# Attention and feed-forward on one core: TensorE's step regrouped into two long fp32r runs, with all queues and the drain reordered

## The chip, the cores and the metric

One core of one Trainium2 chip runs the whole program. The metric is the device time of one execution in microseconds, as the median of several runs. The change touches no arithmetic: the same products are formed in another order.

## What is computed

Input `x` is 128 batches of 32 tokens with 512 features, 4096 tokens in all. Cut to what matters:

```python
# style: one 32x32 matrix per batch, picked by a style number
h = einsum('bct,bcd->bdt', x, weights[style])
q, k, v = split(clip(h @ w_qkv.T, -8, 8))        # 32 heads of 16
q, k = layer_norm(q), layer_norm(k)
p = softmax(where(causal, q @ k.T / 4 + alibi, -inf))
x = x + (p @ v) @ w_out.T
# adapter: one 512x512 matrix per batch, picked by an adapter number
y = einsum('bsi,boi->bso', x, weight[adapter])
shared = relu(y @ up) ** 2 @ down
routed = (y @ fc1 @ expert) * sum(top2(y @ gate)) @ fc2
x = x + layer_norm(shared + routed)
```

## The kernel before

Engines: TensorE (PE) multiplies, VectorE (DVE) and ScalarE (ACT) read PSUM and round, GpSimd (POOL) works in SBUF only and issues the gathers and scatters, SyncE (SP) issues the other transfers. Each engine's queue is written out by hand; between them stand semaphores, and `upto(e, name, t)` makes engine `e` wait until event `name` has happened for tile `t`.

The tokens are sorted by style into 32 tiles of 128 (`T = 32`), and by adapter into 38 slots of 128. An fp32 product is made of three fp32r products (high with high, high with low, low with high), each 128x128 by 128x512. In the program's words ACT makes the high part (`high_...`), DVE or POOL the low part (`low_...`).

**The attention stage** is a software pipeline over `i`. In step `i` TensorE forms, for several tiles at once: `style(i+1)`; the three projections `project(i, ...)` (Q, K and V, 12 fp32r matmuls each, L586); `values(i-4)` (L604, 96 small bf16 matmuls); `turn_slot` (transposes of gathered rows, L663) and `adapt_slot(i-6)` (12 fp32r matmuls, L677); `turn_values(i-4)` (L616), `turn_qk(i-1)` twice (L636); `scores(i-2)` (L651, 96 small bf16 matmuls); `out_project(i-4)` (12 fp32r matmuls, L628). Values and scores are each issued as two halves of 48 matmuls, put between fp32r groups. The PSUM banks are `B2` (Q, adapter), `B3` (K, Q turned), `B4` (values turned), `B5` (V, K turned), `B6` (output projection), `B7` (style, slot turned) and `pair` (scores, values).

The chain of one tile behind TensorE: scores, `bias_max` (DVE L1215, L1219), `subtract_max` (POOL L1559), `soft_exp` (ACT L963), `turn_probs` (DVE L1287), `high_probs` (ACT L968) and `low_probs` (POOL L1571), values, `divide` (DVE L1236, L1240), `turn_values`, `high_o` and `low_o`, output projection, `add_x` (x1). The heads' K and V are spread into block form by SP (`spread_k` to `kx`, `spread_v` to `vx`). In the background 20 chunks of feed-forward weights are split into high and low parts and kept in memory (`load_chunk`, `high_chunk`, `low_chunk`, `keep_chunk`), and the adapted rows are scattered to `y_rows`.

**The drain** is what follows step 31: the last tiles' scores, values and output projections, with the first five `up` groups of the feed-forward stage between them. **The feed-forward stage** runs over 8 groups of 512 tokens: 8 times `up` (L741), `gate_products` of the next group (L710), 4 times `down` (L758, L765), and two adapter slots per group. The rows of a group come transposed in halves of 16 bits (`load_y`), are joined to words (`join_y`), and are split (`high_y` on ACT, `low_y` on DVE) before `up` and `gate_products` of that group can run. In group 0 the splits of group 1 are spread over `up` 5, 6 and 7:

```python
        return {5: (0,), 6: (1,), 7: (2, 3)}[f]
```

## Time and profile before

| | us |
|---|---|
| median of 3 runs | 1157.25 (1157.22 to 1161.35) |
| profiled execution | 1158.09 |
| its span, first to last instruction | 1156.3 |
| TensorE busy in the span | 1113.8 (96%) |
| GpSimd, VectorE, ScalarE busy | 709.5, 679.8, 604.2 |
| mean granted TensorE clock | 0.989 |

The profiled execution took 1158.09 us, 1.8 us more than its span; it is 0.84 us above the median of the runs. Matmuls overlap, so a busy TensorE is not one at its peak: the distances between starts tell what a matmul costs in a row of them. The attention stage with its start fills the first 604 us, the drain lies between 604 and 650 us, and from there the feed-forward groups follow.

### The profile page before, as it was taken

How to read it: one execution, taken by the hardware profiler on the slowest of the kernel's cores; microseconds unless marked ns; L12 is line 12 of the kernel's file. 1: busy time of each engine (PE TensorE's matmuls, PEld its weight loads, DVE VectorE, ACT ScalarE, POOL GpSimd, SP SyncE). 2: the span in 40 equal slices, each digit the busy share in tenths (PEclk: the TensorE clock that was granted, in tenths of full speed). 3: DMA queues.
4: the chain of work that ended last, by engine and by line, in shares of the span. 5: the costliest groups of instructions: out<-in, count | busy, mean ns of one | idle time of the engine just before them, and what ended most of it. 6: DMA issues, size and time to landing. Idle time of an engine off the chain costs nothing.

```text
span 1156.3 us, 27340 instructions
## 1 busy us (share of the span) xinstructions
PE 1113.8 (96%) x10996; PEld 885.7 (77%) x10996; DVE 679.8 (59%) x1050; ACT 604.2 (52%) x1009; POOL 709.5 (61%) x610
## 2 busy tenths in 40 slices
PE   6999999999999999999998889999999999999994
PEld 4777777777777777777776668787888878787883
DVE  5767565756575657565667336655656556554532
ACT  4466767676767676757575532516162534424120
POOL 3466787878787878787764445645545454533332
PEclk9999999999999999999998989999999999999998
DMA  6135545454545454436468923241513313130101
GB/s 260 39 95 177 203 158 195 161 201 157 200 158 199 160 197 149 156 125 166 122 189 196 325 90 92 79 140 55 140 65 99 89 67 104 40 83 28 46 28 36
DMA packets 90796, 152.38 MB, mean 132 GB/s; under 512 B 46000, under 2 KB 46768, under 8 KB 85296
## 3 DMA queue, kind: packets, MB, share of 16 engines
q1 hardware_dynamic: 73024, 105.84, 28.8%
q0 software_dynamic: 12224, 34.10, 9.1%
q10 hardware_dynamic: 5424, 10.71, 2.7%
q8 instruction: 88, 1.44, 0.5%
q14 instruction: 36, 0.29, 0.1%
HBM read 89.78 MB, written 38.27 MB: 111 GB/s over the span
## 4 chain that ended last, share of the span: by engine, by line
PE 92%; DVE 3%; DMA 2%; ACT 1%; issue 1%; POOL 1%; SPq 0%; DVEq 0%; ACTq 0%; POOLq 0%
PE bank L586 22%; PE pair L765 15%; PE bank L741 14%; PE bank L677 9%; PE bank L628 8%; PE bank L758 8%; PE bank L576 3%; PE pair L651 3%; PE pair L604 3%; PE bank L636 2%; PE bank L663 2%; PE bank L710 1%; PE bank L616 1%; DMA x_rows<-x1t 1%; DMA stage<-in_wqkv 0%
## 5 line engine op out<-in xcount | busy, mean ns | idle before, releaser
L1565 POOL TENSOR_TENSOR w_lo<-w2t,w_hi 128x2048 fp32r<-128x2048 f32 x38 | 175.5, 4619 | 8.1 <-ACT w_hi L910 7.9
L586 PE MATMUL bank<-wqkv_hi,h_hi 128*128 128x512 f32 x384 | 158.8, 414 | 0.5 <-issue 0.4
L1619 POOL TENSOR_TENSOR u_lo<-act,u_hi 128x512 fp32r<-128x512 f32 x64 | 82.8, 1294 | 112.1 <-ACT u_hi L1097 112.0
L586 PE MATMUL bank<-wqkv_hi,h_lo 128*128 128x512 f32 x384 | 150.6, 392 | 0.0
L586 PE MATMUL bank<-wqkv_lo,h_hi 128*128 128x512 f32 x384 | 149.6, 390 | 0.0
L741 PE MATMUL bank<-yT_hi,up_hi 128*128 128x512 f32 x256 | 101.1, 395 | 0.3 <-DVE yT_lo L1259 0.3
L765 PE MATMUL pair<-down_hi,u_hi 128*128 128x512 f32 x256 | 100.9, 394 | 0.0
L765 PE MATMUL pair<-down_hi,u_lo 128*128 128x512 f32 x256 | 100.8, 394 | 0.0
L765 PE MATMUL pair<-down_lo,u_hi 128*128 128x512 f32 x256 | 100.3, 392 | 0.0
L741 PE MATMUL bank<-yT_lo,up_hi 128*128 128x512 f32 x256 | 99.8, 390 | 0.0
L741 PE MATMUL bank<-yT_hi,up_lo 128*128 128x512 f32 x256 | 99.7, 390 | 0.0
L1422 DVE TENSOR_TENSOR act<-act 128x512 f32<-128x512 f32 x59 | 67.5, 1143 | 50.2 <-ACT act L1093 50.2
L1657 POOL TENSOR_SCALAR fve<-fmv 128x1 f32<-128x1 f32 x32 | 22.8, 712 | 115.6 <-DVE fmv L1477 115.5
L1187 ACT ACTIVATE total<-bank,weight 128x512 f32<-128x512 f32 x32 | 21.9, 684 | 126.6 <-PE bank L758 126.6
L1559 POOL TENSOR_TENSOR probs<-probs,row_max 128x1024 f32<-128x1024 f32 x32 | 61.2, 1911 | 40.4 <-DVE row_max L1219 40.3
L586 PEld LDWEIGHTS bank<-wqkv_hi,h_lo 128*128 128x128 f32 x384 | 72.0, 188 | 16.5
L586 PEld LDWEIGHTS bank<-wqkv_hi,h_hi 128*128 128x128 f32 x384 | 72.2, 188 | 16.0 <-issue 1.7
L586 PEld LDWEIGHTS bank<-wqkv_lo,h_hi 128*128 128x128 f32 x384 | 72.4, 189 | 13.0 <-issue 0.2
L910 ACT ACTIVATE w_hi<-w2t 128x2048 fp32r<-128x2048 f32 x38 | 73.3, 1930 | 13.4 <-DMA w2t<-in_w 13.3
L1571 POOL TENSOR_TENSOR p_lo<-probsT,p_hi 128x1024 bf16<-128x1024 f32 x32 | 68.8, 2150 | 15.3 <-ACT p_hi L968 14.6
L1093 ACT ACTIVATE act<-bank 128x512 f32<-128x512 f32 x64 | 37.8, 591 | 71.0 <-PE bank L741 70.8
L1472 DVE TENSOR_TENSOR total<-total,pair 128x512 f32<-128x512 f32 x32 | 21.9, 684 | 89.4 <-PE pair L765 89.4
(179 smaller groups left out, 2965.8 us busy)
## 6 DMA issues: line engine op xcount, KB each, us to landing
w2t<-in_w SPq DMA_DIRECT2D x38, 1024.0 KB, 4.8
vx<-v_hl SPq DMA_DIRECT2D x128, 68.0 KB
x_rows<-x1t SPq DMA_DIRECT2D x32, 256.0 KB, 3.0
x1g<-x_rows SPq DMA_DIRECT2D x32, 256.0 KB, 3.1
kx<-k_hl SPq DMA_DIRECT2D x124, 64.0 KB
ffn_high<-w_high SPq DMA_DIRECT2D x20, 256.0 KB, 3.1
ffn_low<-w_low SPq DMA_DIRECT2D x20, 256.0 KB, 3.0
stage<-in_wqkv SPq DMA_DIRECT2D x3, 1024.0 KB, 7.9
```

The lines of the kernel that those rows point to most:

```text
L586: m = e.matmul(into, a[:, c, :], b[:, n, c, :], start=(c == 0 and k == 0), stop=(c == KC - 1 and k == 2))
L628: m = e.matmul(B6, a[:, j, :], b[:, j, :], start=(j == 0 and k == 0), stop=(j == BPT - 1 and k == 2))
L677: m = e.matmul(into, a[:, P * c:P * c + P], b[:, c, :], start=(c == 0 and k == 0), stop=(c == KC - 1 and k == 2))
L741: i = e.matmul((B2, B3)[n % 2], a[:, w, cols], b[m % 2][:, c, :], start=(c == 0 and k == 0), stop=(c == KC - 1 and k == 2))
L758: i = e.matmul((B6, B7)[n % 2], a[m % 2][:, c, toks], b[:, c, :], start=(c == 0 and k == 0), stop=(c == KC - 1 and k == 2))
L765: i = e.matmul(pair[:, n % 2, :], a[f][:, toks], b[:, f, :], start=(f == 0 and k == 0), stop=(f == FC - 1 and k == 2))
L910: e.activation(w2_hi[:, :, :], w2t[:, :, :], ACT.Copy).then_inc(d_whi, 1)
L1422: e.tensor_tensor(act[n % 2][:, :], act[n % 2][:, :], act[n % 2][:, :], ALU.mult) \
L1559: e.tensor_tensor(probs[:, :, :], probs[:, :, :], row_max[:, :].rearrange("p (h o) -> p h o", o=1) .broadcast_to([P, HEADS, SEQ]), ALU.sub ...
L1565: e.tensor_tensor(w2_lo[:, :, :], w2t[:, :, :], w2_hi[:, :, :].bitcast(F32), ALU.subtract).then_inc(d_wlo, 1)
L1571: e.tensor_tensor(p_lo[:, :], probsT[:, :], p_hi[:, :], ALU.subtract).then_inc(A["plo"], 1)
L1619: e.tensor_tensor(u_lo[n % FC][:, :], act[n % 2][:, :], u_hi[n % FC][:, :].bitcast(F32), ALU.subtract) \
```

## The change

TensorE's step `i` now reads: Q, K, V projections of tile `i` in a row (36 fp32r matmuls); `turn_slot(i-6)`, `turn_values(i-4)`, `turn_q(i-1)`, `turn_k(i-1)`; `style(i+1)`; the whole of `scores(i-2)`; `adapt_slot(i-6)` and `out_project(i-4)` in a row (24 fp32r matmuls); the whole of `values(i-3)`, which was `values(i-4)` in the middle of the step. Style moves from bank `B7` to `B6`. The loop has one step fewer, step 31 being written into the drain. The core of the diff, TensorE first:

```diff
-            def values(t, half):
+            def values(t):
-            def scores(t, half):
+            def scores(t):
...
+            for i in range(T - 1):
+                project_q(i)
+                if i < SHORT:
                     style(i + 1)
...
+                project_k(i)
+                project_v(i)
+                if i >= LAG:
                     turn_slot(i - LAG, B7)
+                if i >= 4:
                     turn_values(i - 4)
+                if i >= 1:
+                    turn_q(i - 1)
+                    turn_k(i - 1)
+                if i >= SHORT:
+                    style(i + 1)
+                if i >= 2:
+                    scores(i - 2)
+                if i >= LAG:
                     adapt_slot(i - LAG, B2)
+                if i >= 4:
                     out_project(i - 4)
+                if i >= 3:
+                    values(i - 3)
```

The drain on TensorE after the change:

```python
project_q(T - 1); project_k(T - 1); project_v(T - 1)
turn_slot(LAST, B7); turn_values(T - 5); turn_k(T - 2); turn_q(T - 2)
scores(T - 3); adapt_slot(LAST, B2)
turn_qk(T - 1, q ...); turn_qk(T - 1, k ...)
values(T - 4); out_project(T - 5); turn_values(T - 4); scores(T - 2)
out_project(T - 4); values(T - 3); up(0, 0); turn_values(T - 3)
scores(T - 1); up(0, 1); values(T - 2); out_project(T - 3)
turn_values(T - 2); up(0, 2); out_project(T - 2); values(T - 1)
up(0, 3); turn_values(T - 1); up(0, 4); out_project(T - 1)
gate_products(0)
```

The other queues follow. POOL's step:

```diff
             for i in range(T):
+                upto(e, "o", i - 4)
+                if i > LAG:
+                    scatter_slot(i - LAG - 1)
...
+                if i + 3 < T:
+                    gather_x(i + 3)
+                    gather_style(i + 3)
+                if i >= LAG:
+                    low_w2(i - LAG)
+                reciprocals(i)
+                if i >= 3:
+                    low_probs(i - 3)
+                if i >= LAG - 1:
+                    upto(e, "s", i - 2)
+                    gather_slot(i - LAG + 1)
+                if i >= 2:
+                    subtract_max(i - 2)
+                low_v(i)
+                if i + 2 < T:
+                    style(i + 2)
```

VectorE's step becomes: `turn_probs(i-3)`, `divide(i-4)`, clip and statistics of Q, `low_chunk(i-5)`, clip and statistics of K, aggregate, clip of V, `low_slot`, `low_o(i-4)`, `low_h(i+1)`, `bias_max(i-2)`, `low_q` and `low_k(i-1)`, `add_x(i-4)`. ScalarE's: `high_probs(i-3)`, `high_w2`, `high_chunk(i-5)`, `normalize(i-1)`, `slot_in`, `high_o(i-4)`, `high_v(i)`, `high_h(i+1)`, scaling and high parts of Q and K of tile `i-1`, `slot_out`, `soft_exp(i-2)`. SP's: `spread_v(i-3)`, `store_x1(i-5)`, `keep_chunk(i-5)`, `load_chunk(i-4)`, `load_w2(i-5)`, `spread_k(i-1)`.

For group 1 the words are joined by VectorE in the drain, into a region of their own (`words_second`, laid over `yt`), and all four splits follow `up` 5 of group 0:

```diff
-        return {5: (0,), 6: (1,), 7: (2, 3)}[f]
+        return range(KC) if f == EARLY else ()
...
+            for c in range(KC):
+                join_y(1, c)
+            add_x(T - 2)
             divide(T - 1)
```

What that moves, in the queues as they are built. TensorE before, from the V projection of a middle step to the next step's first projection (L586 projection, L616 values turned, L636 Q or K turned, L677 adapter, L651 scores, L628 output projection, L576 style, L604 values):

```order
L663 MATMUL bank<-cst,xg 128x128 x4
...
L616 MATMUL bank<-cst,on 128x128 x4
L636 MATMUL bank<-cst,qn 128x128 x4
L677 MATMUL bank<-w_hi,xgT_hi 128x512
...
L636 MATMUL bank<-cst,kn 128x128 x4
L651 MATMUL pair<-kx,q_hi 32x128 x8
...
L628 MATMUL bank<-wo_hi,o_hi 128x512
...
L576 MATMUL bank<-style_bd,xt 128x128 x4
```

TensorE after the change, the same place (L592 projection, L667 slot turned, L620 values turned, L640 Q and K turned, L582 style, L654 scores, L681 adapter):

```order
L592 MATMUL bank<-wqkv_hi,h_lo 128x512
L667 MATMUL bank<-cst,xg 128x128 x4
L620 MATMUL bank<-cst,on 128x128 x4
L640 MATMUL bank<-cst,qn 128x128 x4
L640 MATMUL bank<-cst,kn 128x128 x4
L582 MATMUL bank<-style_bd,xt 128x128 x4
L654 MATMUL pair<-kx,q_hi 32x128 x8
...
L681 MATMUL bank<-w_hi,xgT_hi 128x512
```

All turns, style and the scores now stand in one stretch between the two fp32r runs; the adapter moved behind the scores.

ScalarE before, in group 0 from the copy of the gates on (L1093 relu, L948 words joined, L953 high part of the words, L1097 high part of u, L906 slot in):

```order
L959 ACTIVATE gates<-bank 16x512
L1093 ACTIVATE act<-bank 128x512
L948 ACTIVATE y_words<-yt_first 128x512 x2
L953 ACTIVATE yT_hi<-y_words 128x512
L1097 ACTIVATE u_hi<-act 128x512
L906 ACTIVATE xgT_hi<-bank 128x512
```

ScalarE after the change, the same place (L1103 relu, L969 high part of the words, L1107 high part of u, L920 slot in, L975 gates):

```order
L975 ACTIVATE gates<-bank 16x512
L1103 ACTIVATE act<-bank 128x512
L969 ACTIVATE yT_hi<-words_second 128x512 x4
L1107 ACTIVATE u_hi<-act 128x512
L920 ACTIVATE xgT_hi<-bank 128x512
```

The joining has left ScalarE here, and all four high parts of group 1 stand behind the first relu.

## Rows read from the trace of the kernel before

**Rows 1.** The page's chain that ended last: shares of the span by engine

```profile
PE 92%; DVE 3%; DMA 2%; ACT 1%; issue 1%; POOL 1%; SPq 0%; DVEq 0%; ACTq 0%; POOLq 0%
```

**Rows 2.** Windows: length, busy time of PE, PEld, DVE, ACT, POOL; granted clock, DMA

```profile
120.00:604.00 484.00, 483.74 (x6945) 384.71 (x6943) 311.09 (x526) 326.89 (x562) 386.56 (x318) 1.00 0.52 171
```

**Rows 3.** TensorE's waits: us in total, times, longest

```profile
PE bank L710 <- DVE yT_lo L1259: 5.3, 1, 5.3
PE pair L651 <- DVE on L1240: 3.9, 1, 3.9
PE pair L604 <- DVE probs L1215: 2.3, 1, 2.3
...
PE bank L677 <- DVE xgT_lo L1208: 1.5, 1, 1.5
PE pair L604 <- POOL p_lo L1571: 1.0, 1, 1.0
```

**Rows 4.** Timeline of TensorE, a middle step: start, length, instruction, count

```profile
412.50 0.47 PE L586 MATMUL bank<-wqkv_hi,h_hi 128*128 128x512 f32 x1
...
415.44 0.22 PE L604 MATMUL pair<-vx,p_hi 128*32 128x68 bf16 x4
...
416.00 0.47 PE L586 MATMUL bank<-wqkv_hi,h_hi 128*128 128x512 f32 x1
...
418.93 0.22 PE L604 MATMUL pair<-vx,p_hi 128*32 128x68 bf16 x4
...
419.44 0.66 PE L663 MATMUL bank<-cst,xg 128*128 128x128 f32 x4
...
426.33 0.60 PE L636 MATMUL bank<-cst,kn 128*128 128x128 f32 x4
426.86 0.25 PE L651 MATMUL pair<-kx,q_hi 64*32 64x128 bf16 x8
...
427.39 0.50 PE L628 MATMUL bank<-wo_hi,o_hi 128*128 128x512 f32 x1
...
430.38 0.25 PE L651 MATMUL pair<-kx,q_hi 64*32 64x128 bf16 x8
...
430.95 1.13 PE L576 MATMUL bank<-style_bd,xt 128*128 128x128 f32 x8
431.84 0.48 PE L586 MATMUL bank<-wqkv_hi,h_hi 128*128 128x512 f32 x1
```

**Rows 5.** Timeline of TensorE: whole bursts, scores at the start, values in the drain

```profile
53.65 0.25 PE L651 MATMUL pair<-kx,q_hi 64*32 64x128 bf16 x8
...
54.58 1.16 PE L576 MATMUL bank<-style_bd,xt 128*128 128x128 f32 x8
...
632.32 0.39 PE L628 MATMUL bank<-wo_hi,o_lo 128*128 128x512 f32 x1
632.64 0.22 PE L604 MATMUL pair<-vx,p_hi 128*32 128x68 bf16 x4
...
633.54 0.50 PE L741 MATMUL bank<-yT_hi,up_hi 128*128 128x512 f32 x1
```

**Rows 6.** Timeline of TensorE: step 31 begins, gate products end, first down begins

```profile
585.63 0.47 PE L586 MATMUL bank<-wqkv_hi,h_hi 128*128 128x512 f32 x1
...
649.43 0.40 PE L710 MATMUL bank<-yT_lo,gate_hl 128*16 128x512 f32 x1
...
672.81 0.78 PE L758 MATMUL bank<-route_hi,yT_hi 128*128 128x512 f32 x1
```

**Rows 7.** Windows as rows 2: a stretch without fp32r at the start, two after waits

```profile
52.60:55.50 2.90, 2.90 (x115) 2.59 (x112) 2.41 (x7) 1.90 (x5) 0.88 (x3) 1.00 0.03 6
...
612.20:615.20 3.00, 2.61 (x101) 2.04 (x101) 2.86 (x4) 1.14 (x4) 0.00 (x0) 0.50 0.90 77
...
668.70:673.80 5.10, 5.09 (x14) 2.73 (x15) 0.00 (x0) 1.46 (x2) 3.15 (x3) 0.50 0.33 102
```

**Rows 8.** Timeline of ScalarE in the drain: four high parts of words

```profile
607.14 2.18 ACT L953 ACTIVATE yT_hi<-words_first 128x512 fp32r<-128x512 f32 x4
```

More of the change, by code:

```diff
@@ L377, in words @@
     def words(m, c):
-        return y_words[m % 2][:, c, :] if m else words_first[:, UP_CHUNKS // KC * c + 1, :]
+        if m == 0:
+            return words_first[:, UP_CHUNKS // KC * c + 1, :]
+        return words_second[:, c, :] if m == 1 else y_words[m % 2][:, c, :]
     def halves(word, n):
@@ L403, in route_bank @@
     def route_bank(c):
-        return pair[:, 0, :] if c == 0 else B6
+        return pair[:, 0, :] if c == 0 else B7
     def last_slot(m):
@@ L783, in _, with project_q @@
                          start=True, stop=True)
-            e.matmul(B6[0:1, 0:SLOTS], idc[:, :], onehot[:, 0::BPT], start=True, stop=True) \
+            e.matmul(B7[0:1, 0:SLOTS], idc[:, :], onehot[:, 0::BPT], start=True, stop=True) \
                 .then_inc(s_tp, 1)
             make_route(0)
-            for i in range(T):
-                live = lambda t: 0 <= t < T
-                slot = i >= LAG
-                if 0 < i < T - 1:
-                    style(i + 1)
-                if live(i):
-                    upto(e, "cq", i - 1)
-                    if i > LAG:
-                        e.wait_ge(d_mc, i - LAG)
-                    project(i, 0, B2, "pq")
-                if i == 0:
-                    style(1)
+            def project_q(i):
+                upto(e, "cq", i - 1)
+                if i > LAG:
+                    e.wait_ge(d_mc, i - LAG)
+                project(i, 0, B2, "pq")
@@ L845, in _ @@
+            turn_q(T - 2)
+            scores(T - 3)
+            adapt_slot(LAST, B2)
+            e.wait_ge(d_tl, LAST + 1)
+            turn_qk(T - 1, qn[(T - 1) % 2], "qn", B7, "tq")
+            upto(e, "khi", T - 2)
+            upto(e, "klo", T - 2)
+            turn_qk(T - 1, kn[(T - 1) % 2], "kn", B5, "tk")
+            values(T - 4)
+            out_project(T - 5)
             turn_values(T - 4)
+            scores(T - 2)
+            out_project(T - 4)
+            values(T - 3)
             up(0, 0)
-            out_project(T - 4)
@@ L848, in _ @@
-            values(T - 3, 0)
-            values(T - 3, 1)
+            turn_values(T - 3)
+            scores(T - 1)
             up(0, 1)
-            turn_values(T - 3)
-            scores(T - 1, 0)
-            scores(T - 1, 1)
+            values(T - 2)
+            out_project(T - 3)
+            turn_values(T - 2)
             up(0, 2)
-            out_project(T - 3)
-            values(T - 2, 0)
-            values(T - 2, 1)
+            out_project(T - 2)
+            values(T - 1)
             up(0, 3)
-            turn_values(T - 2)
@@ L860, in _ @@
-            values(T - 1, 0)
-            values(T - 1, 1)
-            out_project(T - 2)
             turn_values(T - 1)
@@ L1404, in _ @@
                 m.then_inc(A["aggr"], 1)
-                if 0 <= i - 4 < CHUNKS:
-                    low_chunk(i - 4)
-                if i == T - 1:
-                    e.wait_ge(f_y, 2 * KC * 16)
-                    for c in range(KC):
-                        join_y(c)
-                if live(i - 4):
+            for i in range(T - 1):
+                if i >= 3:
+                    turn_probs(i - 3)
+                if i >= 4:
+                    divide(i - 4)
+                take_q(i)
+                if i < SHORT:
+                    low_h(i + 1)
+                stats_of(i, 0, qn, "cq")
+                if i == 0:
+                    low_weights(3)
+                if 0 <= i - 5 < CHUNKS:
+                    low_chunk(i - 5)
+                take_k(i)
+                stats_of(i, 1, kn, "ck")
+                aggregate(i)
+                take_v(i)
+                if i >= LAG:
+                    low_slot(i - LAG, B7)
+                if i >= 4:
+                    low_o(i - 4)
+                if i >= SHORT:
+                    low_h(i + 1)
+                if i >= 2:
+                    bias_max(i - 2)
+                if i >= 1:
+                    low_q(i - 1, B3)
+                    low_k(i - 1, k_bank(i - 1), k_hl)
+                if i >= 4:
                     add_x(i - 4)
@@ L1607, in _, with low_v @@
                     .then_inc(A["shift"], 1)
+            def low_v(t):
                 upto(e, "vhi", t)
```

421 lines of the change are left out of this document (201 added, 220 removed).

## The prediction

> **What bounds the kernel now.** I read the chain of waits first: TensorE holds 92% of it, every other engine 3% or less [rows 1]. The windows say where: in the 484 us from 120 to 604 TensorE is busy for 483.74, GpSimd for 386.56, ScalarE for 326.89 and VectorE for 311.09 [rows 2]. So the attention stage has no wait to remove; there only what TensorE itself spends can change the time. The table of TensorE's waits then shows what is left outside that stage: 5.3, 3.9, 2.3, 1.5 and 1.0 us, each a single wait [rows 3]. By the timeline they lie between 604 and 669 us, in the drain and in group 0 of the feed-forward stage. Last, the timeline of one middle step: it lasts 431.84 - 412.50 = 19.34 us [rows 4]. The reader should see the distances between starts there. Twelve fp32r matmuls in a row stand about 0.23 us apart, but each passage to the small bf16 matmuls and back costs something over the matmuls themselves.
>
> **Part one, the regrouped step.** The count of matmuls stays the same, and so does the price of each. What goes is the halving of two bursts. Values: in the step the first half takes 416.00 - 415.44 = 0.56, the second 419.44 - 418.93 = 0.51 [rows 4]. A whole burst between two fp32r groups, in the drain, takes 633.54 - 632.64 = 0.90 [rows 5]. Going in costs 632.64 - 632.32 = 0.32 where the distance is otherwise 0.23, so 0.09 more, and the first fp32r matmul behind a burst has a distance about 0.1 longer. Two halves: 0.56 + 0.51 + 2 x 0.09 + about 0.1 = 1.35; one whole 0.90 + 0.09 + 0.1 = 1.09. That is 0.26 saved. Scores: the halves take 427.39 - 426.86 = 0.53 and 430.95 - 430.38 = 0.57 [rows 4], the whole 54.58 - 53.65 = 0.93 [rows 5]; with one entry (0.09) and one return (0.1) fewer, 0.17 + 0.19 = 0.36 is saved. The transposes cost the same 0.36 to 0.44 per group wherever they stand, beside fp32r or beside each other; so moving them is free. One passage is new, from style to bf16: the trace never has it. Its nearest row is the K transposes before scores, 426.86 - 426.33 = 0.53 [rows 4], about 0.1 above a group before other fp32 work; it may cost nothing, or 0.2. With 0.05 for it, I take 0.26 + 0.36 - 0.05 = 0.57 a step; the ends are 0.35 (my entry and return costs are seen only once each) and 0.70. Steps 4 to 30 have all of it: 27 x 0.57 = 15.4 us, from 9.5 to 19. The new step is 18.77 us. Values of tile 0 move from step 4 into step 3, and the last ones out of the drain; what one end gains the other pays.
>
> **Does anything else hold that step up?** I laid the queues out along one new step, 0 at its first Q matmul, with the durations of the trace: Q, K, V end at 8.4, the turns at 10.2, style at 11.2, scores at 12.1, adapter and output projection at 17.7, values at 18.7. VectorE: clip of V done at 9.2, and the K turn into the same bank starts at 9.7, a margin of 0.5 and the tightest of all. `bias_max` ends at 15.1. GpSimd starts at 0.2 (values of the step before), then scatter, two gathers, the adapter's low part (until 8.7), reciprocals, `low_probs` (12.4), one gather (13.7), then `subtract_max` from 15.1 to 17.1, `low_v` and style, end 18.7. It has 0.2 us to the next step, but 1.4 us of wait inside, so a late start is taken up. ScalarE ends with the exponential at 18.2. The exponential, the turn of the probabilities and both parts of them reach values with 5 us to spare. SP spreads K when its low part is there (16.7) and has until 12 of the next step. Each of these is hidden behind 18.77 us of TensorE; its cover is gone if the step falls below about 18.6. In front of the loop little changes; I put the start at zero, with 1 us either way.
>
> **Part two, the drain.** From step 31's first matmul to the end of the gate products of group 0 there are 649.66 - 585.63 = 64.0 us (the last gate matmul starts at 649.43 [rows 6]). Three waits, 3.9 + 2.3 + 1.0 = 7.2 us [rows 3], go in the new order, since more independent work stands before the last turns. With them goes the clock's fall: in 612.2 to 615.2, right behind the waits, the granted clock is 0.50, which is 1.2 GHz, against 1.00 (2.4 GHz) [rows 7]. Half of 3.0 us is 1.5. Step 31 also has its two halvings less, 0.6. Together 9.3. Laying the new queues out the same way gives new waits: `turn_values(28)` waits 0.35 for the quotient, which stands behind the word splits on VectorE; `out_project(28)` 1.0 for its low part, behind the exponential and the scaling of K on ScalarE; `scores(31)` waits for the spread K of the last tile, issued after its low part at 24.9 us from the start of step 31, over 2.5 us of issue and perhaps 2 of landing, 0.7 to 2, say 1. That is 2.3. Net 7.0 us; the ends are 1 (each new wait tripled) and 9.3.
>
> **Part three, group 0.** Before, `gate_products(1)` waited 5.3 us for the last low part of group 1's words [rows 3], because ScalarE joined and rounded them between the relus. The clock then stood at 0.50 for 5.1 us [rows 7], half of it lost: 2.5. Now VectorE joins them in the drain, and ScalarE's four high parts behind the first relu take 2.2 us [rows 8]. They are done some 6 us after the gate products of group 0, while TensorE comes to `gate_products(1)` only 13.6 us after them. So 5.3 + 2.5 = 7.8 goes. The 1.5 us for the adapter's low part [rows 3] stay: ahead of it ScalarE waits for the store of the last x1, and the four high parts fit in front of that store. What is late next is the weight transfer for `down`, or the low part of the adapter in `down` (about 1.4 us of margin after the transfer of its matrix); the first `down` starts today at 672.81 [rows 6]. So the ends are 4.5 and 7.8. From there to the end nothing changes but one store.
>
> **The sum.** 15.4 + 7.0 + 7.8 = 30.2 us. The profiled execution has 1158.09, which gives 1127.9; it stands 0.84 above the median, so on the scale of the runs 1157.25 - 30.2 = 1127.0. The parts' best ends, 19 + 9.3 + 7.8 = 36 and 1 for the start, give 1120; their worst, 9.5 + 1 + 4.5 = 15, give 1142.
>
> **The rivals.** *The drain keeps its waits in new places* (0.15). Against: the layout above. For: it is five hand-written queues, and one instruction late on any of them stops TensorE; a stop of a few us brings the clock's fall with it, as behind the waits of the old drain. Then part two is worth nothing or minus 3, and part three half: 1127 + 7 + 4 = 1138, 1134 to 1143.
>
> *Another engine sets the step* (0.12). GpSimd has 386.56 us of work in 484 [rows 2], 15.4 per 19.34 us step, plus its issue gaps; it now starts only when the previous values are done, and the softmax chain is tied to two waits inside the step. If the step stays at 19.34 us, the 15.4 us go: 1142. It takes 30.2 / 27 = 1.1 us of wait per step to lose everything. I put this between 1139 and 1155.
>
> *The clock falls in every step* (0.09), the way to slower. Before, no stretch without fp32r matmuls inside the steps is longer than scores and style, 431.84 - 430.38 = 1.46 us [rows 4], and the longest at the start, 2.9 us of turns, scores and style, ran at 1.00 [rows 7]. Now turns (4 x 0.44), style (1.0) and scores (0.9) stand together: 3.7 us in each step without one. Falls so far followed only idle time, and TensorE is not idle here; this speaks against it. If it fell, each would cost between the two losses seen, 1.5 and 2.5 us [rows 7]: 27 x 1.5 - 30 gives +10, 27 x 2.5 - 30 gives +38, so 1167 to 1195. It decides from 1.1 us per step on. The Trainium skill ("TensorE: Matmul & The Clock Gate", Part 4, PE-mode transpose) says that transposes don't count as TensorE activity the way matmuls do, so by that rule a stretch opened by four groups of transposes is where the clock would give way. By the rule the kernel would be slower than before, at about the 1167 to 1195 of this rival; the start's stretch at 1.00 is the only trace against it.
>
> **How the numbers follow.** The forecast, 1120 to 1134 about 1127, has 0.63; the drain 0.15, the engine-bound step 0.12, the clock 0.09, and 0.01 is left. The range leaves out the clock and the tail of the engine-bound step: 1118 to 1146. A measurement of this kernel tells about 0.5% from no change, 5.8 us. All of the forecast, the drain and most of the engine-bound step are faster by more: 0.87. Within 0.5%: 0.04. Slower: the clock, 0.09.
>
> **What would show it.** In the new profile: the middle step at 18.7 to 18.9 us between first Q matmuls, with the distance 0.23 unbroken over 36 matmuls; granted clock 1.00 from 120 to 585; no wait of TensorE in it for POOL or VectorE; step 31 to gate products in 56 to 58 us; no wait of `gate_products(1)` and no window at 0.50 behind it; the 1.5 us for the adapter still there. A step over 19.1 us, a clock under 0.95 in the attention stage, or drain waits over 6 us in sum would prove me wrong.

## The result and the profile after

| | before | after |
|---|---|---|
| median of 20 runs each, us | 1157.74 (1156.88 to 1161.35) | 1162.42 (1156.93 to 1171.22) |
| profiled execution, its span | 1158.09, 1156.3 | 1165.9, 1164.1 |
| mean granted clock | 0.989 | 0.986 |

The change makes the kernel slower, by a ratio of 1.0047 (95% interval 1.0029 to 1.0064), and its runs spread over 14 us, those of before over 4.5. The profiled execution of the change is one of the longer ones, 3.5 us above its median; the stretches below are of that one execution. Four marks in TensorE's timeline cut the two spans into five stretches: the first Q matmul of step 4, that of step 31, the last gate matmul of group 0 and the first routed product (the marks of the last three of before are in [rows 6]).

| stretch, us | before | after | difference | forecast |
|---|---|---|---|---|
| start, to step 4 | 68.33 | 80.45 | +12.12 | 0 |
| steps 4 to 30 | 517.30 | 513.12 | -4.18 | -15.4 |
| drain, to the last gate matmul | 63.80 | 68.97 | +5.17 | -7.0 |
| group 0, to its first routed product | 23.38 | 18.80 | -4.58 | -7.8 |
| the rest | 483.49 | 482.76 | -0.73 | 0 |

These add up to 7.8 us, the difference of the spans. The gains in the steps and in group 0 are there in part, and the start and the drain lost. First the chain that ended last in the changed kernel:

```profile
PE 84%; DMA 6%; issue 4%; DVE 4%; ACT 1%; SPq 1%; POOL 0%; DVEq 0%; POOLq 0%
```

TensorE had 92% of it [rows 1]; now transfers, issue and VectorE hold 14%, where they had 6. The windows (columns as in [rows 2]) show the attention stage and five short stretches behind waits:

```profile
120.00:590.00 470.00, 461.99 (x6771) 383.37 (x6771) 310.77 (x511) 325.24 (x560) 379.40 (x315) 1.00 0.54 170
607.00:612.00 5.00, 4.65 (x110) 3.96 (x111) 2.88 (x6) 4.16 (x10) 3.56 (x5) 0.66 0.62 161
634.00:638.00 4.00, 3.56 (x102) 2.98 (x103) 1.97 (x3) 0.00 (x0) 0.00 (x0) 0.57 1.09 337
672.00:677.00 5.00, 4.86 (x15) 3.94 (x16) 0.38 (x1) 1.03 (x2) 1.28 (x1) 0.68 0.00 0
36.00:41.00 5.00, 3.72 (x14) 3.40 (x15) 4.77 (x4) 1.64 (x3) 3.22 (x4) 0.66 0.21 59
65.00:72.00 7.00, 6.98 (x18) 4.62 (x19) 2.67 (x4) 3.14 (x5) 2.05 (x2) 0.57 0.49 142
```

In 470 us of attention TensorE was idle for 8, where it had been idle for 0.3 in 484 [rows 2]; the clock stayed at 1.00 there. Behind the long waits at the start, in the drain and in group 0 it fell; a value like 0.66 is the mean of a part at 0.50 (1.2 GHz) and a part at 1.00 (2.4 GHz). TensorE's table of waits over the whole span names what it waited for:

```profile
PE bank L582 <- issue: 8.4, 3, 4.3
PE bank L640 <- DVE vf L1222: 7.8, 7, 4.5
PE pair L654 <- DMA kx<-k_last: 4.3, 1, 4.3
PE bank L681 <- DVE xgT_lo L1233: 2.8, 1, 2.8
```

Compare [rows 3]: the waits of 5.3, 3.9 and 2.3 us are gone, three groups that were not there have come, and the adapter's 1.5 us have grown to 2.8. Each has its own cause.

**The start: GpSimd's style comes last in its step.** `issue` in the first row hides a wait for GpSimd. Timeline of GpSimd, then of TensorE, around the style product of tile 2:

```profile
34.19 0.23 POOL L1630 TENSOR_SCALAR var_eps<-mean_var 128x2 f32<-128x2 f32 x1 [7.07 <-DVE mean_var L1418]
...
35.65 1.12 POOL L1646 TENSOR_TENSOR v_hl<-vf,v_hl 128x512 bf16<-128x512 f32 x1
36.73 0.45 POOL L1552 TENSOR_TENSOR style_bd<-style_rows,cst 128x128 f32<-128x128 f32 x1
```

```profile
37.28 0.98 PE L582 MATMUL bank<-style_bd,xt 128*128 128x128 f32 x3 [4.28 <-issue]
```

The style operand needs nothing of the softmax chain, but it now stands in the queue behind the variance, for which GpSimd waited 7.07 us, and behind the low part of V. It ends at 37.18, and TensorE starts at 37.28 after 4.28 us idle. At tile 4 it happens again (3.2 us). The clock windows 36 to 41 at 0.66 and 65 to 72 at 0.57 are what follows.

**The steps: the w2 transfer shares its time with the spreads.** Undisturbed steps last 18.7 to 18.9 us, as forecast, but 10 of the 24 from step 7 on are over 19.0, up to 20.77. SP's timeline of one such step, then ScalarE's:

```profile
305.20 0.34 SPq L448 DMA_DIRECT2D w2t<-in_w  x1
305.72 3.52 SPq L501 DMA_DIRECT2D kx<-k_hl  x4
309.35 2.89 SPq L510 DMA_DIRECT2D vx<-v_hl  x4
```

```profile
313.62 1.92 ACT L924 ACTIVATE w_hi<-w2t 128x2048 fp32r<-128x2048 f32 x1 [3.40 <-DMA w2t<-in_w]
```

1 MB is issued at 305.20, the small pieces of both spreads right behind it, and ScalarE gets the matrix at 313.6, 8.4 us after its issue. Behind `w_hi` on ScalarE stand the feed-forward chunk and the scaling of Q and K; VectorE's `w_low` and V's clip come late in turn, and TensorE's K turn waits for that clip (seven waits in the second row above, six of them in the steps). From 120 to 590 us ScalarE waits 14 times for this matrix, 20.7 us in sum. In the trace of before it never does there: that order issues the w2 transfer by itself, behind the spreads.

**The drain: VectorE's joins meet GpSimd's long low part.** Timelines of VectorE and GpSimd:

```profile
597.91 5.85 DVE L1280 COPY words_first<-yt_first 128x512 uint16<-128x512 uint16 x4
603.66 0.67 DVE L1222 TENSOR_SCALAR kn<-bank 128x512 f32<-128x512 f32 x1
...
605.25 1.43 DVE L1280 COPY words_first<-yt_first 128x512 uint16<-128x512 uint16 x4
606.58 0.68 DVE L1222 TENSOR_SCALAR vf<-bank 128x512 f32<-128x512 f32 x1
```

```profile
598.62 4.82 POOL L1620 TENSOR_TENSOR w_lo<-w2t,w_hi 128x2048 fp32r<-128x2048 f32 x1 [3.13 <-ACT w_hi L924]
```

Four copies of halves to words take 1.43 us when GpSimd's long subtraction isn't running, 5.85 when its 4.82 us subtraction runs: the longest single one of the eight lasts 4.83 us, where their median is 0.45, and the four end 0.3 us after the subtraction ends (603.44). So one of them stood still for it. The Trainium skill ("SBUF — State Buffer", "SBUF: two separate sides") says that VectorE and GpSimd share one pair of ports to SBUF, and calls it "an exclusive lock, not a bandwidth split"; these rows agree. V's clip ends at 607.26 and TensorE's K turn starts at 607.31, after 4.45 us. Then the spread K of tile 31 (issued 624.70 to 627.91) meets the 2 MB of the odd half of the up weights, which ScalarE's queue issues at 626.62 and 627.02: 4.3 us.

One more stop of the drain isn't a wait for an operand. TensorE stops in the middle of a burst of values, whose operands it had waited for at the burst's start:

```profile
641.74 0.21 PE L609 MATMUL pair<-vx,p_lo 128*32 128x68 bf16 x2 [1.47 <-issue]
```

A like one, of 1.29 us, stands in the scores of step 6. A transfer of the DMA kind "instruction" stands in the DMA view of both places; the profile names no releaser, so the cause is not shown.

**Group 0.** The gate products of group 1 wait for nothing. But VectorE has all four low parts in a row now, and the adapter's stands behind them:

```profile
667.62 3.56 DVE L1287 TENSOR_TENSOR yT_lo<-words_second,yT_hi 128x512 fp32r<-128x512 f32 x4
671.10 0.68 DVE L1233 TENSOR_TENSOR xgT_lo<-bank,xgT_hi 128x512 fp32r<-128x512 f32 x1
```

so its wait grew from 1.5 [rows 3] to 2.8 us, with a window at 0.68 behind it. This fall of the clock isn't there in every execution: in the traces of two experiments below, e1 and e5, the same wait is followed by a clock of 1.00, and group 0 lasts 17.4 us in place of 18.8.

### The profile page after: what moved, and what is told of

Same layout as the page of the kernel before. It is cut to its first block, busy times and chain, and to the rows that moved or that the text cites. A ratio compares the mean times of both kernels' runs of the same rounds, so it can differ in the third digit from the quotient of the medians.

```text
span 1164.1 us, 27353 instructions
## 1 busy us (share of the span) xinstructions
PE 1103.2 (95%) x10996; PEld 895.4 (77%) x10996; DVE 696.3 (60%) x1058; ACT 602.2 (52%) x1001; POOL 711.1 (61%) x610
## 4 chain that ended last, share of the span: by engine, by line
PE 84%; DMA 6%; issue 4%; DVE 4%; ACT 1%; SPq 1%; POOL 0%; DVEq 0%; POOLq 0%
PE bank L592 18%; PE pair L768 15%; PE bank L744 15%; PE bank L681 9%; PE bank L761 8%; PE bank L632 6%; DMA w2t<-in_w 4%; PE bank L582 3%; PE pair L654 2%; PE bank L640 2%; PE pair L609 2%; PE bank L714 1%; PE bank L667 1%; PE bank L620 1%; DVE words_first L1280 1%
## 5 line engine op out<-in xcount | busy, mean ns | idle before, releaser
L592 PE MATMUL bank<-wqkv_hi,h_hi 128*128 128x512 f32 x384 | 154.8, 403 | 0.3
L592 PE MATMUL bank<-wqkv_lo,h_hi 128*128 128x512 f32 x384 | 150.0, 391 | 0.0
L592 PE MATMUL bank<-wqkv_hi,h_lo 128*128 128x512 f32 x384 | 149.9, 390 | 0.0
L592 PEld LDWEIGHTS bank<-wqkv_hi,h_hi 128*128 128x128 f32 x384 | 72.5, 189 | 17.6 <-issue 1.4
L592 PEld LDWEIGHTS bank<-wqkv_hi,h_lo 128*128 128x128 f32 x384 | 72.4, 188 | 15.4
L592 PEld LDWEIGHTS bank<-wqkv_lo,h_hi 128*128 128x128 f32 x384 | 72.5, 189 | 15.0 <-issue 1.2
L1103 ACT ACTIVATE act<-bank 128x512 f32<-128x512 f32 x64 | 37.8, 591 | 75.2 <-PE bank L744 75.1
```

The costliest lines, as they stand in the source:

```text
L592: m = e.matmul(into, a[:, c, :], b[:, n, c, :], start=(c == 0 and k == 0), stop=(c == KC - 1 and k == 2))
```

## The experiments

Medians stand with their ratio to the kernel before on the same chip. All but e4 and e8 mend one or more of the places above; "drain" is the stretch of the table. The stretches come from one profiled execution each. Where the drain's queues are those of the change (e1, e3, e5), it lasts 68.95, 68.91 and 68.75 us, as against 68.97; the steps differ more from trace to trace: 513.12 after the change, 520.67 in e1 and 507.58 in e2, with the same queues.

**e1_style_first.** In GpSimd's loop:

```diff
+                if i < SHORT:
+                    style(i + 2)
                 upto(e, "o", i - 4)
...
-                if i + 2 < T:
+                if SHORT <= i < T - 2:
                     style(i + 2)
```

> The changed kernel, with GpSimd's style of tiles 2 to 5 put back to the front of its steps 0 to 3, as it stood before. Theory (the start lost 11 us because TensorE's style(2) and style(4) wait for GpSimd, whose own style now stands behind the reciprocals and the subtraction of the same step): step 4 begins near 70 us instead of 80.45, the waits of 4.3 and 3.2 us before style are gone, and the time falls by 8 to 11 us. Rival (the start is bound by the new place of the values and the later projections): step 4 begins after 77 us and the time falls by less than 3 us.

Measured: 1159.56 us, ratio 1.0007 (0.9989 to 1.0025), a gain of 3 to 5 us and not of 8 to 11. Step 4 begins at 72.70 (80.45 after the change, 68.33 before), and of the 8.4 us of `issue` waits 1.0 is left. So the order on GpSimd cost 7.8 us in the start. Steps 4 to 30 of this trace take 520.67 us, 7.6 more than after the change with the same queues, and ate that gain. A wait stays at the end of step 3, which the old order had not:

```profile
71.79 0.22 PE L609 MATMUL pair<-vx,p_hi 128*32 128x68 bf16 x4 [2.48 <-POOL p_lo L1626]
```

The values of tile 0 had moved into step 3, and their probabilities are not ready there.

**e2_join_later.** VectorE's joins go between later instructions, and on SP the spread K of tile 30 goes ahead of the word loads of group 1:

```diff
-            join_y(0, 0)
-            join_y(0, 1)
...
-            join_y(0, 2)
-            join_y(0, 3)
             take_v(T - 1)
+            join_y(0, 0)
             low_slot(LAST, B7)
             low_o(T - 5)
+            join_y(0, 1)
             low_k(T - 2, B5, k_hl)
             bias_max(T - 3)
+            join_y(0, 2)
+            join_y(0, 3)
```

> The changed kernel; in the drain VectorE joins the words of group 0 behind the clips of K and V of tile 31, no longer between them, ScalarE's high parts follow, and the spread of K of tile 30 goes ahead of the transposed loads. Theory (the joins ran 4 us long beside GpSimd's low part of the adapter matrix and held up the clip of V): the wait of 4.45 us before the last K turns is gone, and step 31 to the gate products shrinks from 69.2 to 62 to 65 us. Rival (the joins take as long wherever they stand, and what follows them on VectorE is late instead): at most 2 us of the 69.2 go.

Measured: 1158.15 us, 1.0011 (0.9984 to 1.0038); drain 66.06 against 68.97, a gain of 2.9 us, between what the theory and the rival gave. The 4.5 us for V's clip are gone. In their place stand 3.2 us for the quotient `on`, since the last four joins took 4.24 us beside GpSimd's subtraction of the maximum and low part of V:

```profile
PE bank L620 <- DVE on L1265: 3.2, 1, 3.2
PE pair L654 <- issue: 2.9, 1, 2.9
```

The second row is again a stop in the middle of a burst, the scores of tile 31.

**e3_w2_alone.** SP waits for the w2 transfer before it issues the spreads:

```diff
                     load_w2(i - 5)
+                    e.wait_ge(d_w2, 16 * (i - 4))
```

> The changed kernel with one wait more on SP: the spreads of K and V are issued only when the adapter matrix has landed. Theory (the matrix lands late in some steps because eight spread transfers with small packets are issued right behind it and share the DMA engines): from issue to landing under 6 us in every step, ScalarE's waits for it go, steps 7 to 30 all take 18.8 to 19.0 us, 5 to 8 us are saved and the runs lie closer together. Rival (something else holds the slow steps, chunks or x1): steps of 19.3 us and more stay, gain under 2 us, or the later spreads stall scores.

Measured: 1156.46 us, 0.9984 (0.9974 to 0.9994), as the theory said, and the runs lie within 3.1 us, not 14. Steps 7 to 30 last 18.71 to 18.89 us but for one of 19.04; the median is 18.76. One added wait on SP makes the kernel 6 to 7 us faster (by the medians, by the ratios), and ScalarE's waits for the matrix from 120 to 590 us fall from 20.7 to 4.4 us. The same step as above, SP and ScalarE:

```profile
299.69 0.35 SPq L448 DMA_DIRECT2D w2t<-in_w  x1
304.58 2.41 SPq L501 DMA_DIRECT2D kx<-k_hl  x4
```

```profile
304.62 1.90 ACT L925 ACTIVATE w_hi<-w2t 128x2048 fp32r<-128x2048 f32 x1
```

The matrix is there within 4.9 us of its issue, not 8.4, and the four pieces of K issue in 2.41 us, not 3.52. Not every slow step goes with it: in e6 and e7, which have the same wait on SP, three steps each last 19.0 to 20.3 us. Why is not shown.

**e4_w2_behind.** The other cure: ScalarE takes `w_hi` behind the chunk and the scaling, so that a late matrix stops nobody:

```diff
-                if i >= LAG:
-                    high_w2(i - LAG)
                 if 0 <= i - 5 < CHUNKS:
                     high_chunk(i - 5)
                 if i >= 1:
                     normalize(i - 1)
+                if i >= LAG:
+                    high_w2(i - LAG)
```

> The changed kernel with ScalarE's high part of the adapter matrix behind the chunk and the normalizing instead of in front of them. Theory (a late matrix costs because ScalarE's chunk, which VectorE's clips of K and V stand behind, queues behind it): the waits before the K turns (3.4 us in sum from 120 to 590 us) go; the low part on GpSimd now comes later, so where the matrix was early nothing is lost, and 0 to 5 us are saved. Rival (GpSimd's low part sets the adapter's start): TensorE waits at the adapter in every step by 0.3 to 1 us, and the kernel is 8 to 25 us slower.

Measured: 1168.99 us, 1.0095 (1.0078 to 1.0112). TensorE's waits of the attention stage:

```profile
PE bank L681 <- POOL w_lo L1620: 12.8, 19, 1.1
```

The late matrix then stops TensorE itself, through GpSimd's low part, in 19 steps. That is the rival's mechanism, at about 6 us instead of its 8 to 25. The order stays, and what has to change is the transfer.

**e5_start.** e3 and e1, and the values of tile 0 back in step 4:

```diff
             for i in range(T - 1):
                 project_q(i)
+                if i == 4:
+                    values(0)
...
-                if i >= 3:
+                if i >= 4:
                     values(i - 3)
```

> The changed kernel with the transfer of w2 alone on its queue, GpSimd's style of tiles 2 to 5 at the front of steps 0 to 3, and the values of tile 0 back in step 4, between its Q and K projections. Theory (the start lost its 12 us to two orders: style last on GpSimd, and values of tile 0 asked for a step too early, 2.5 us of wait for p_lo): step 5 begins at 87 to 90 us (before 86.3, after 98.4), no wait of values in step 3, and the time is 1145 to 1150 against 1156.5 with w2 alone. Rival (the start is bound by the first Q, K, V loads or by the turns' new place): step 5 begins at 93 or later and the time is 1152 or more.

Measured: 1145.99 us, 0.9887 (0.9871 to 0.9904). Step 4 begins at 69.81 (80.45 after the change) and step 5 at 88.82 (98.37). At step 4, 10.6 of the 12.1 us are back; 1.1 of these is only the work of values, done in step 4 again, which now lasts 19.01 us, not 17.92. So both orders together cost about 9.5 us. The other 1.5 are not explained; with these same queues step 4 begins anywhere from 67.53 to 70.24 us in the traces of e7 and e9 to e14.

**e6_kx_and_slot.** e3, the odd up weights behind the last spread K, and the adapter's slot between the words of group 1:

```diff
-        return range(KC) if f == EARLY else ()
+        return {EARLY: (0, 1), EARLY + 1: (2, 3)}.get(f, ())
...
-            e.wait_ge(S["lo"], KC)
-            fetch_up(m_up[1], 0, 1, 8)
-            fetch_up(m_up[1], 1, 1, 8)
             high_o(T - 3)
             high_probs(T - 2)
+            e.wait_ge(S["lo"], KC)
+            upto(e, "kx", T - 1)
+            fetch_up(m_up[1], 0, 1, 8)
+            fetch_up(m_up[1], 1, 1, 8)
```

> The changed kernel with w2 alone on its queue; the fetch of the odd half of the up weights (2 MB) issued only when the last spread K has landed; in group 0 two turned words, then the adapter's slot, then two more. Theory: the 4.3 us of scores(31) for kx go to under 1 and the window behind it stays at a clock of 1.00; the adapter's 2.8 us go to under 0.5 and its window stays at 1.00; together 8 to 11 us, time 1146 to 1149. Rival for the first (the spread is late by its own small packets and its issue, not by the fetch): the wait of 4.3 stays within 0.5, or the wait moves to the up projections that need the odd half. Rival for the second: the adapter waits for ScalarE's high part instead, over 1.5 us. With one rival true the time is near 1151, with both 1156.

Measured: 1152.03 us, 0.9939 (0.9923 to 0.9956), not the 1146 to 1149 of the theory. Group 0 fell from 18.74 to 15.29 us: forecast 23.38 - 7.8 = 15.6, and the adapter waits 0.7. The drain did not gain (68.12):

```profile
PE pair L610 <- issue: 3.7, 1, 3.7
```

No wait for kx (the edit moves not only the fetch but also `high_o` and `high_probs` ahead of it), but one of 3.7 us in front of the values of tile 31. The profile names no releaser for it, but its other operands were there long before: GpSimd's low part of the probabilities ends at 636.09, the wait at 641.58. And ScalarE, whose next transfer waits for the same spread V, issues it at 641.46. So it is the spread V of tile 31, issued from 632.50 to 635.35; that the 2 MB of ScalarE's queue (from 624.09 on) delay it is argued, not shown, since 1 MB of the down weights is issued beside it at 632.69.

**e7_all.** e5, e6, and the joins spread further over VectorE's queue, with the matching high parts on ScalarE, and SP as in e2:

```diff
-            join_y(0, 0)
-            join_y(0, 1)
...
-            join_y(0, 2)
-            join_y(0, 3)
             take_v(T - 1)
             low_slot(LAST, B7)
             low_o(T - 5)
+            join_y(0, 0)
             low_k(T - 2, B5, k_hl)
             bias_max(T - 3)
-            low_y(0, 0)
             low_q(T - 2, B3)
-            low_y(0, 1)
-            low_y(0, 2)
             divide(T - 4)
             turn_probs(T - 3)
             add_x(T - 5)
+            join_y(0, 1)
             low_o(T - 4)
             bias_max(T - 2)
             low_k(T - 1, B5, k_last)
+            join_y(0, 2)
+            join_y(0, 3)
+            low_y(0, 0)
...
```

> All the mended orders together: w2 alone, style first in steps 0 to 3, values of tile 0 in step 4, odd fetch behind the last spread K, slot between the words of group 1, and VectorE's joins of the first words spread behind quotient, K and output parts that TensorE waits for. Theory: the losses are independent and lie one behind the other in time, so they add: 1156.5 less 9 (start) less 10 (kx and slot) less 4 to 7 (the wait for V's clip 4.5 us and its clock) is 1130 to 1136, near the 1127 that the layout of the queues promised. Rival (a wait taken away comes back at the next tight place of the drain): over 1141.

Measured: 1142.95 us, 0.9859 (0.9839 to 0.9879): the rival, by 2 us over its bound of 1141. Drain 65.80. The waits for V's clip and kx are gone and one for vx of tile 29 has come:

```profile
PE pair L610 <- DMA vx<-v_hl: 6.7, 1, 6.7
```

**e8_values_halved.** e3 with `values` in two halves of 48 matmuls, half of `out_project` between:

```diff
-                    out_project(i - 4)
-                    values(i - 3)
+                    out_project(i - 4, lambda: values(i - 3, 0))
+                    values(i - 3, 1)
```

> The changed kernel with w2 alone, and in steps 5 to 30 the values burst cut into two halves with half of the output projection between. Theory (a halving costs one more passage in and out, 0.26 us by the prediction's first term): the steps of 18.77 become 19.0 to 19.05, and the time 1162 to 1164 against 1156.5. Rival (the gain of the step came from the transposes standing together, not from whole bursts): steps stay at 18.8 and the time at 1156 to 1157.

Measured: 1164.63 us, 1.0047 (1.0030 to 1.0064). The time is 0.6 us over the range of the theory. The steps last 19.01 to 19.17 us, median 19.07 against 18.76: one halving costs 0.31 us, forecast 0.26. So whole bursts do pay, and not only transposes that stand together. Starts in TensorE's timeline of one step:

```profile
417.27 0.22 PE L611 MATMUL pair<-vx,p_hi 128*32 128x68 bf16 x4
417.78 0.50 PE L637 MATMUL bank<-wo_hi,o_hi 128*128 128x512 f32 x1
...
419.37 0.22 PE L611 MATMUL pair<-vx,p_hi 128*32 128x68 bf16 x4
419.93 0.47 PE L593 MATMUL bank<-wqkv_hi,h_hi 128*128 128x512 f32 x1
```

The halves take 0.51 and 0.56 us, as in [rows 4].

**e9_joins_spread and e10_and_kx.** e7 with SP's order as in the change and w2 of the first late slot behind three more spreads; the odd fetch at the change's place (e9) or behind kx (e10):

```diff
             load_y(1, (0, 1))
             spread_k(T - 2)
-            load_w2(slot_up(0))
             spread_v(T - 3)
...
             store_x1(T - 4)
+            load_w2(slot_up(0))
             load_y(1, (2, 3))
```

> As the kernel with all mended orders, but SP keeps the change's own order (words of group 1 ahead of the spread K of tile 30), the w2 transfer of the first late slot goes behind three more spreads, and the odd half of the up weights is fetched where the change fetches it. Theory (in the kernel with all mended orders the 6.7 us for vx of tile 29 came from SP: the transposing load held its queue for 9.5 us, and 1 MB of w2 was issued 0.5 us ahead of that spread): the wait for vx is gone, step 31 to the end of the gate products takes 60 to 63 us (66.0 there, 69.2 after the change), of it up to 4.3 us for kx of tile 31, and the time is 1134 to 1139. Rival (the drain's spreads are slow wherever they stand): a wait for kx or vx over 5 us stays, and the time is 1142 or more.

> As e9_joins_spread, and the odd half of the up weights is fetched only behind the last spread K. Theory (large transfers and spreads share the DMA engines, and whichever small one stands behind a large one is late): no wait for kx, and a wait of 1 to 4 us for vx of tile 31 in its place, as in e6_kx_and_slot; time 1131 to 1137, within 3 us of e9_joins_spread. Rival (the fetch can be had for nothing once it stands behind kx): the drain takes 57 to 59 us and the time is 1128 to 1131.

Measured: 1146.69 us, 0.9895 (0.9878 to 0.9911), drain 72.21; and 1146.44 us, 0.9909 (0.9886 to 0.9931), drain 70.82. Both theories fell. e9's rival held in its numbers, but not in its reason, that the spreads are slow wherever they stand. TensorE waits for the spread K of tile 30, and SP's own timeline says why:

```profile
PE pair L655 <- DMA kx<-k_hl: 7.9, 1, 7.9
```

```profile
585.88 13.76 SPq L486 DMA_TRANSPOSE yt_first<-y_rows  x4
599.75 2.43 SPq L501 DMA_DIRECT2D kx<-k_hl  x4
```

```profile
SPq L486 <- DVE words_first L1283: 8.1, 1, 8.1
```

The word loads of group 1 write the tile that the joins of group 0 read. A join that VectorE does later holds SP, and behind SP stands the spread. So the joins that were moved out of the clips' way came back through another queue. Behind it `up` waits 3.7 us for the low part of the words (1.0 after the change), which the moved joins make late.

**e11_words_last and e12_words_last_fetch_early.** e10 and e9 with all word loads of group 1 behind the spreads of tiles 30 and 31, save the last V:

```diff
-            load_y(1, (0, 1))
             spread_k(T - 2)
...
-            load_y(1, (2, 3))
+            load_y(1, range(KC))
             spread_v(T - 1)
```

> As e10_and_kx, with all four word loads of group 1 on SP behind the spreads of tiles 30 and 31 but the last. Theory (these loads wait for VectorE's joins of the words of group 0, since they write the same tile; SP stands behind them, so a late join is a late spread K): the wait of 7.9 us for kx is gone with its slow clock, and the 3.7 us for yT_lo behind it shrink; step 31 to the end of the gate products takes 56 to 59 us, which is what was forecast for the change, and the time is 1130 to 1135. Rival (every gain in the drain is paid back at the next place): a new wait over 4 us, for vx of tile 31 or for the words of group 1, and the time stays at 1141 to 1146.

> As e11_words_last, but the odd half of the up weights is fetched at the change's own place, not behind the last spread K. Theory: the 2 MB lie beside the last spread again, scores(31) waits 3 to 4.5 us for kx with 1 to 2 us of slow clock; time 4 to 6 us over e11_words_last. Rival (without the word loads in the queue the spread has landed before the fetch begins): no wait, and the same time within 1.5 us.

Measured: 1142.76 us, 0.9870 (0.9836 to 0.9904), drain 69.68; and 1146.66 us, 0.9882 (0.9859 to 0.9906), drain 71.63. The theory of e11, a drain of 56 to 59 us and a time of 1130 to 1135, fell, and its rival held. The wait for kx is gone in both, so e12's mechanism was wrong: its fetch is issued at 608.96, 2.5 us behind the last piece of the spread K, where in the changed kernel it was issued between the pieces. Its median is 3.9 us more, but the intervals overlap. In front of the values of tile 31 stand 4.9 and 6.5 us: the spread V waits behind the word loads.

```profile
607.52 13.91 SPq L486 DMA_TRANSPOSE yt_first<-y_rows  x8
621.54 3.07 SPq L510 DMA_DIRECT2D vx<-v_hl  x4
```

```profile
629.86 0.37 ACTq L946 DMA_DIRECT2D route_hi<-ffn_high  x1
```

```profile
629.98 0.22 PE L609 MATMUL pair<-vx,p_hi 128*32 128x68 bf16 x4 [4.93 <-issue]
```

As in e6, ScalarE's transfer and TensorE's values wait for the same spread and go on together, in e11 as shown and in e12 at 635.84 and 635.96. A second wait is the price of the late joins, in e11:

```profile
PE bank L744 <- DVE yT_lo L1290: 4.8, 1, 4.8
```

**e13_second_words.** e11 with half of the word loads behind that spread, the joins of group 1 behind the last low part:

```diff
-            load_y(1, range(KC))
+            load_y(1, (0, 1))
             spread_v(T - 1)
             store_x1(T - 3)
+            load_y(1, (2, 3))
```

> As e11_words_last, with half of the word loads of group 1 behind the last spread V on SP, and VectorE's joins of these words behind the last low part of the output. Theory (values(31) waited 4.9 us there because its spread stood behind 13.9 us of transposing loads): that wait goes to under 1 us with its slow clock, the 4.8 us for yT_lo stay, step 31 to the last gate product takes 62 to 65 us (69.7 in e11_words_last) and the time is 1135 to 1139. Rival (the drain pays every gain back at the next place): another wait over 3 us comes up behind it, for the odd half of the up weights or the last output part, and the time stays within 2 us of 1142.8.

Measured: 1144.24 us, 0.9874 (0.9852 to 0.9896). The drain fell to 63.61 us as expected, and group 0 rose from 15.39 to 21.52:

```profile
PE bank L668 <- DVE x1t L1278: 5.7, 1, 5.7
PE bank L745 <- DVE yT_lo L1291: 4.8, 1, 4.8
```

The last x1 now stands behind the joins, and the turn of the slot waits for it. The time is the rival's again, not the 1135 to 1139 of the theory.

**e14_no_drain_edit.** e5 and e6 together: the joins and SP's drain as in the change.

> w2 alone, the two mends of the start, the odd fetch behind the last spread K, and the slot between the words; the joins of the first words and SP's drain stand as in the change. Theory: the mends outside the drain add, 1146.0 of e5_start less 3.5 for the adapter's wait in group 0, and in the drain the wait for kx is exchanged for one for vx: 1141 to 1144, the same as the kernels with reordered joins, so these orders of the drain brought nothing. Rival (the reordered joins did bring 4 to 7 us): 1147 or more.

Measured: 1139.86 us (1137.82 to 1142.27), 0.9842 (0.9820 to 0.9865), the lowest median of all and faster than both kernels; its interval overlaps those of e7, e11 and e13, which have other orders of the joins, so these orders brought nothing that the runs can show. The mends add, to a little more than forecast: start 69.72, steps 4 to 30 504.87, drain 64.53, group 0 15.23. The drain still has the 4.5 us for V's clip; in place of 4.3 for kx there are 1.3 for vx of tile 30, and the 1.5 of `issue` are a stop inside the same burst:

```profile
PE bank L641 <- DVE vf L1226: 4.5, 1, 4.5
...
PE pair L610 <- issue: 1.5, 1, 1.5
PE pair L610 <- DMA vx<-v_hl: 1.3, 1, 1.3
```

The drain's queues are those of e6, where it took 68.12 us. The 3.7 us for vx of tile 31 are not there in this trace.

## Why the prediction was wrong

Forecast 1127.0, range 1118 to 1146, measured 1162.42. The count of what TensorE does was right, and the layout of the other queues was not. The errors below are those of the profiled execution, 1165.9 against 1127.9: 12.1 + 11.2 + 12.2 + 3.2, less 0.7 in the rest, are 38.0 us.

**"That is 0.57 a step", right.** With w2 alone on its queue the step lasts 18.76 us, forecast 18.77; e8 puts one halving back for 0.31, forecast 0.26. The sum of that term is not clean: it counts one return for the two halves of values, where each half has one. With two it is 0.36. By difference the scores with the one new passage are worth 0.27, where the forecast had 0.31; no run halves them alone. So that 18.77 was met so closely is partly luck, by under 0.1 us. In the changed kernel itself 14 of the 24 steps last 18.71 to 18.89.

**"Each of these is hidden behind 18.77 us of TensorE", wrong, 11.2 us.** I laid out SP's spread K as one item with a term and left out that the change also puts the w2 transfer directly ahead of both spreads. ScalarE's `w_hi` was in no line of the layout as a thing that could be late. e3 gave 7.9 us of it back in steps 4 to 30 (513.12 to 505.18). Of the 3.3 us that e3 still lacks of the forecast, 0.9 were never to be had, since step 30 of before lasted only 18.45 us, and 1.6 are step 6, at 20.56, with the 1.3 us stop inside its scores.

**"I put the start at zero, with 1 us either way", wrong, 12.1 us.** The step was forecast from a steady state. In the first steps there is no backlog: an operand that waits at the end of GpSimd's queue is waited for, and the values of a tile one step earlier meet probabilities that aren't ready. e1 shows 7.8 us for the first, e5 2.9 more for the second, 1.1 of which is the work of values that moved back to step 4. The prediction gave no reason for its zero.

**Part two, the drain, wrong by 12.2 us.** That the old waits would go was right (7.2 us). Of the three new ones, `turn_values(28)` was 0.35 in the forecast and 0.91 in the trace, `out_project(28)` 1.0 and 0.74, kx of tile 31 "0.7 to 2, say 1" and 4.3. Missing was the largest, 4.5 us for V's clip: the joins were taken at the 2.8 us for eight that the trace of before shows, without asking what GpSimd would do beside them. Missing too was the odd half of the up weights as a neighbour of the last spread, and the clock's fall behind both (0.66 and 0.57, 1.7 us lost each), and the stop of 1.5 us inside a burst. This was the rival "the drain keeps its waits in new places", at 0.15. Its words fit; its price did not, since it put part two at nothing or minus 3, where minus 5.2 was measured, and its 1134 to 1143 left out the losses of the start and the steps. Nine kernels with other orders of the drain, from 63.6 to 72.2 us, never came near the forecast 57 us.

**Part three, group 0, right in mechanism, 3.2 us short.** The 5.3 us and their slow clock went. "The 1.5 us for the adapter's low part stay" failed: four low parts on VectorE in a row made them 2.8, and behind them 1.6 us went in a window at 0.68 of the clock (not so in e1 and e5). With the slot between the words (e6) group 0 takes 15.29 us, forecast 15.6.

**The rivals.** "Another engine sets the step": not GpSimd, whose 386 us were counted, but a transfer that another engine waits for, and it took 8 of the 15.4 us, not all. "The clock falls in every step" was wrong: 1.00 over 470 us, with 3.8 us of turns, style and scores in each step. The Trainium skill ("TensorE: Matmul & The Clock Gate", Part 4) says that a transpose doesn't count as a busy TensorE the way a matmul does. Read as in the prediction, the clock would have fallen; with 1.8 us of transposes in such a stretch it didn't. Every fall of the clock in this trace followed an idle TensorE.

What is left open: whether any order of these queues gives a drain near 57 us, what stops TensorE inside a burst, and why the last spreads land late, since each experiment that moved a large transfer in the drain moved other work with it.

## What to carry to other kernels

When a step is regrouped, what TensorE gains can be read from distances between starts, and came out here to 0.05 us for the halving that was tested by itself. What it costs is decided by what each queue has behind an instruction: list for every moved instruction, the transfers too, what waits behind it, and do so for the first steps and the drain apart, since there no backlog hides a wait. Keep a large transfer apart from small urgent ones; here an added wait on the queue that issues both was the faster order.

## What was not expected of the hardware

A copy of 16-bit halves on VectorE and a subtraction on GpSimd exclude each other: 5.85 us for four copies beside 4.82 us of GpSimd, 1.43 without. It works both ways: in the trace of before GpSimd's tiny variance step took 2.66 us beside eight such copies, and 0.23 elsewhere. A 1 MB transfer landed within 4.9 us of its issue alone and 8.4 with two spreads of small pieces behind it. And the clock: in the trace of the change five waits of TensorE, 2.8 to 4.5 us and 19.1 in all, were followed by the five windows above, of 4 to 7 us at 0.57 to 0.68, in which 9.7 us of the clock were lost, about half as much again as the waits. But the price of one wait isn't fixed. The 2.8 us in group 0 cost 1.6 us more in the trace of the change and nothing in that of e5:

```profile
653.00:660.00 7.00, 5.63 (x25) 4.62 (x26) 1.61 (x3) 1.72 (x3) 1.29 (x1) 1.00 0.17 39
```
